# A decoder layer on one Trainium2 core: rows of q and k stacked through memory, the first LayerNorm's rows spread over steps, the cross turn one step later

## The reference

```
x = x + self_attention(layernorm(x))        # Wq, Wk, Wv with biases; 32 query heads, 16 key/value heads of 32, causal
x = x + cross_attention(layernorm(x), ctx)  # no weights; 32 query heads on 8 context heads, 64 context rows, added mask
x = x + ffn(layernorm(x))                   # silu(x Wg^T) * (x Wu^T) Wd^T, hidden size 3584, weights in 4-bit codes x scales
```

## Time and profile before

| | us |
|---|---|
| median of 3 runs (lowest to highest) | 3028.31 (3022.53 to 3028.32) |
| profiled execution, own time | 3025.31 |
| its span | 3023.5 |
| TensorE busy in the span | 2642.9 (87%) |
| VectorE, ScalarE, GpSimd busy | 2079.2, 1569.8, 1225.7 |
| attention, until the last batch's cross part ends | about 1176 |

### The profile page before, as it was taken

One profiled execution on the slowest core, in us unless ns is written; L12 is line 12 of the kernel. 1 busy time (PEld: TensorE's weight loads), 2 busy tenths in 40 slices (PEclk: granted clock), 3 DMA queues, 4 the chain that ended last, 5 costly groups with the idle time before them and its releaser, 6 DMA issues.

```text
span 3023.5 us, 52802 instructions
## 1 busy us (share of the span) xinstructions
PE 2642.9 (87%) x18464; PEld 1414.6 (47%) x18464; DVE 2079.2 (69%) x2844; ACT 1569.8 (52%) x2794; POOL 1225.7 (41%) x1068
## 2 busy tenths in 40 slices
PE   5878877886888653599999999999999999999999
PEld 2555554555655442344444444444444444444444
DVE  5455456546655657687786887878878788787872
ACT  3445444444554534674564745646556465474650
POOL 2345444544554634242442433424334243342430
PEclk9988988997999767799999999999999999999999
DMA  4121112222211214111111211112111111121112
GB/s 157 37 77 45 46 55 65 65 67 66 57 49 50 68 55 140 55 63 47 56 49 42 69 35 56 56 42 63 42 49 56 43 62 49 42 63 42 56 38 111
DMA packets 149813, 180.20 MB, mean 60 GB/s; under 512 B 39920, under 2 KB 91632, under 8 KB 149616
## 3 DMA queue, kind: packets, MB, share of 16 engines
q1 hardware_dynamic: 149616, 177.83, 19.0%
HBM read 132.00 MB, written 25.17 MB: 52 GB/s over the span
## 4 chain that ended last, share of the span: by engine, by line
PE 56%; DVE 2%; issue 1%; ACT 1%; DMA 1%; POOL 0%; SPq 0%; DVEq 0%; ACTq 0%; POOLq 0%
PE f_bank L1462 36%; PE f_down L1482 19%; DVE line L1586 1%; DMA codes<-in_codes 1%; DVE f_stats L1600 0%; DVE fT_l L1613 0%; ACT line L1511 0%; ACT f_xn L1522 0%; ACT fT_h L1530 0%; PE f_down L1444 0%; DVE w L1592 0%; ACT line L1508 0%; DVE h L1622 0%; DVE y L1627 0%; DVE f_mean_var L1603 0%
## 5 line engine op out<-in xcount | busy, mean ns | idle before, releaser
L1586 DVE TENSOR_TENSOR line<-line 128x512 f32<-128x512 f32 x1008 | 928.8, 972 | 43.7 <-issue 29.1
L1511 ACT ACTIVATE line<-codes 128x512 f32<-128x512 int32 x1008 | 590.8, 620 | 386.0 <-DVE line L1586 288.0
L1462 PE MATMUL f_bank<-fT_h,up_h 128*128 128x512 f16 x1792 | 680.9, 380 | 4.3 <-DVE fT_l L1613 3.0
L1462 PE MATMUL f_bank<-fT_l,up_h 128*128 128x512 f16 x1792 | 680.7, 380 | 0.0
L1462 PE MATMUL f_bank<-fT_h,up_l 128*128 128x512 f16 x1792 | 680.4, 380 | 0.0
L510 POOL TENSOR_TENSOR p_l<-p,p_h 128x512 f16<-128x512 f32 x320 | 372.0, 1172 | 452.6 <-ACT p_h L920 451.6
L912 ACT ACTIVATE p<-bank 128x512 f32<-128x512 f32 x320 | 190.6, 596 | 462.7 <-PE bank L704 462.4
L1074 DVE TENSOR_REDUCE block_max<-bank 128x4 f32<-128x512 f32 x320 | 218.7, 686 | 273.2 <-PE bank L675 270.5
L1627 DVE SCALAR_TENSOR_TENSOR y<-f_down,y 128x1024 f32<-128x1024 f32 x224 | 274.3, 1224 | 190.9 <-PE f_down L1482 190.9
L1392 POOL TENSOR_TENSOR up_l<-w,up_h 128x512 f16<-128x512 f32 x112 | 145.0, 1295 | 530.4 <-ACT up_h L1516 530.4
L1387 POOL TENSOR_TENSOR w<-w,scales 128x512 f32<-128x512 f32 x168 | 263.8, 1570 | 227.4 <-DVE w L1592 227.4
(11 more groups left out here) (159 smaller groups left out, 4535.3 us busy)
## 6 DMA issues: line engine op xcount, KB each, us to landing
codes<-in_codes SPq DMA_DIRECT2D x168, 256.0 KB, 3.0
scales<-in_scales SPq DMA_DIRECT2D x336, 128.0 KB, 2.9
xn<-in_x SPq DMA_DIRECT2D x16, 512.0 KB, 4.5
q_rows<-nat_h SPq DMA_DIRECT2D x256, 32.0 KB, 1.9
x_unit<-in_x SPq DMA_DIRECT2D x64, 128.0 KB, 2.7
x<-x_unit SPq DMA_DIRECT2D x64, 128.0 KB, 2.2
y<-x SPq DMA_DIRECT2D x4, 2048.0 KB, 12.8
out<-y SPq DMA_DIRECT2D x16, 512.0 KB, 2.6
```

What stands on the lines that cost most here:

```text
L1462: mm = nc.tensor.matmul(bank[(GATE, UP)[kind] + n % 2][:, :], w[:, chunk, kind, P * c:P * c + P], x[:, c, cols], start=(m == 0), stop=(m = ...
L1511: op = nc.scalar.activation(line[:, m, :], codes[:, slot, :], ACT.Copy, scale=slope, bias=intercept)
L1586: nc.vector.tensor_tensor(line[:, n + 2, :], line[:, n, :], line[:, n + 2, :], ALU.max)\
```

## The change

It has four parts.

1. **Stacking.** `nat` holds both parts of a kind side by side. SyncE stores it as one transfer (`store_nat`, 128 rows x 2 KB) to a tensor in memory, waits, and loads the stacked rows with 3 transfers of 128 KB (32 rows x 4 pairs x 1 KB).
2. **LayerNorm's rows.** `turn_in(s)` replaces `last_turn` and the `FIRST_*` tables. For batch 1 rows are turned in steps 1, 3, 5 and 7 of batch 0; for batch 2 in steps 9 and 13 of batch 0 and 1 and 5 of batch 1; for batch 3 one batch later. A block is turned into `x1T` and stored (`store_turned`, 512 KB) to memory; in i = 9 the four blocks are loaded into `xT` (`load_turned`, 4 x 512 KB) once the batch's projections are done. `xT` is now laid out by block, high and low, column block: a projection's moving operand `xT[:, :, half, c, :]` has four runs of 128 columns. `KINDS_AT` moves a kind: steps 5, 6, 7 have one each and step 8 has one.
3. **Cross turn.** `x_turn`, `x_high_part` and `x_low_part` of piece y = s - 21 stand in chunks 1, 1 and 2 of step s, a step after its scores; `x_weigh` in chunk 3, the output at the end of VectorE's step; the exponential in chunk 3. `T_OF` swaps banks to fit.
4. **Around these.** `p32` has 3 buffers for 4. The x2 store moves from i % 4 = 0 to 1, on GpSimd the shift and the root stand behind more low parts, and at the start all four blocks of rows are loaded and normalised before the weights are cut.

```diff
-        S_OF, T_OF = (0, 0, 1, 0, 1), (1, 1, 0, 1, 0)
+        S_OF, T_OF = (0, 0, 1, 0, 1), (0, 1, 0, 1, 1)
...
-        KINDS_AT = {0: (6,), 1: (7,), 2: (8,), 3: (9,), 4: (10, 11), 5: (12, 13), 6: (14,), 7: (15,)}
+        KINDS_AT = {0: (6,), 1: (7,), 2: (8,), 3: (9,), 4: (10, 11), 5: (12,), 6: (13,), 7: (14,), 8: (15,)}
...
+        def turn_in(s):
             b, i = divmod(s, NP)
+            if 0 < b < B and i % 4 == 3:
+                return "cross", b - 1, i // 4
+            if b == 0 and i in (1, 3, 5, 7):
+                return "first", 1, i // 2
+            if 0 <= b < B - 2 and i in (9, 13):
+                return "first", b + 2, i // 4 - 2
+            if 0 < b < B - 1 and i in (1, 5):
+                return "first", b + 1, 2 + i // 4
+            return None
...
+            def load_turned(b):
+                sp.wait_ge(turned_stored, 16 * TURNED_BY[b])
+                sp.wait_ge(proj_done, NP * b)
+                for i in range(QT):
+                    sp.dma_start(xT[:, i, :, :, :].rearrange("p a c n -> p (a c n)"), dram["xT"][b % 2, i, :, :])\
+                        .then_inc(turned_loaded, 16)
...
+            def store_nat(q):
+                u, kind = q // 4, q % 4
+                sp.wait_ge(proj_low, 3 * u + kind + 1)
+                if u >= 2:
+                    sp.wait_ge(rows_stacked[kind], 16 * 3 * (u - 1))
+                sp.dma_start(dram["nat"][u % 2, kind, :, :], nat[:, kind, :, :].rearrange("p a t -> p (a t)"))\
+                    .then_inc(nat_stored[kind], 16)
...
             def stack_rows(u, kind):
                 if kind == 0 and u >= 2:
                     sp.wait_ge(t_scored, CHUNKS * PAIRS * (u - 1))
-                sp.wait_ge(proj_low, 3 * u + kind + 1)
-                for j in range(4):
-                    for r in range(3):
-                        ...
-                        sp.dma_start(dst, src[D * j:D * j + D, kind, :]).then_inc(rows_stacked[kind], 16)
+                sp.wait_ge(nat_stored[kind], 16 * (u + 1))
+                for r in range(3):
+                    half = (0, 0, 1)[r] if kind == 0 else (0, 1, 0)[r]
+                    ...
+                    src = dram["nat"][u % 2, kind, :, T * half:T * half + T].rearrange("(j d) t -> d j t", d=D)
+                    sp.dma_start(dst, src).then_inc(rows_stacked[kind], 16)
...
                     if k == 1:
                         if s % 2 == 0 and 0 <= s < NS:
                             turn_max(s // 2)
-                        y = crossed(s - 1 - X_LAG, s)
                         if y is not None:
-                            if y >= 1:
-                                pe.wait_ge(x_read, y)
-                            x_weigh(y, XO_BANK, px_h, px_l)
+                            pe.wait_ge(t_exp, min(CHUNKS * (s - 1) + 3, CHUNKS * NS))
+                            if y >= 1:
+                                pe.wait_ge(x_low, y)
+                            x_turn(y, T_BANK + XT_OF, s32[:, y % 2, :])
...
-                    if k == 3 and x is not None:
-                        ...
-                        x_turn(x, T_BANK + XT_OF, s32[:, x % 2, :])
+                    if k == 3 and y is not None:
+                        if y >= 1:
+                            pe.wait_ge(x_read, y)
+                        x_weigh(y, XO_BANK, px_h, px_l)
...
             def exps(f):
                 act.wait_ge(t_scored, f + 1)
-                if f >= 4:
-                    act.wait_ge(p_low, f - 3)
+                if f >= 3:
+                    act.wait_ge(p_low, f - 2)
...
+                    if turn_in(s + 1) and k == 1:
+                        turn_stats(turn_in(s + 1))
+                    if turn_in(s + 1) and k == 4:
+                        ln_normal(LN_AT[turn_in(s + 1)], turn_row(turn_in(s + 1)))
+                if y is not None:
+                    x_out(y, XO_BANK)
```

More of the change, by code:

```diff
@@ L468, in _ @@
             sp.dma_start(t.mask[:, :, :], dram["mask"].rearrange("(r p) t -> p r t", p=P)).then_inc(small_loaded, 16)
-            for n in range(4, 10):
+            for n in range(2, 8):
+                if n < 4:
+                    sp.wait_ge(ln_xn, n + 1)
                 load_w(n)
@@ L472, in _ @@
                 step(s)
-                if s >= FROM:
-                    load_w(16 + s)
+                for n in range(2):
+                    if 8 + 2 * (s - FROM) + n < NW:
+                        load_w(8 + 2 * (s - FROM) + n)
             for u in range(2):
@@ L600, in _ @@
                 if n < NX:
-                    shift(x, p32[:, x % 4, :])
+                    shift(x, p32[:, x % 3, :])
                 if n >= 2:
@@ L645, in project @@
                             pe.wait_ge(w_low, 4 * g + piece + 1)
-                        for m, (w, x) in enumerate(((t.w_h, xT_h), (t.w_h, xT_l), (t.w_l, xT_h))):
-                            mm = nc.tensor.matmul(dst[:, :], w[:, c, cols], x[:, c, :],
+                        for m, (w, half) in enumerate(((t.w_h, 0), (t.w_h, 1), (t.w_l, 0))):
+                            mm = nc.tensor.matmul(dst[:, :], w[:, c, cols], xT[:, :, half, c, :],
                                                   start=(c == 0 and m == 0), stop=(c == CT - 1 and m == 2))
@@ L651, in project @@
                     for c in range(CT):
-                        for m, (w, x) in enumerate(((t.w_h, xT_h), (t.w_h, xT_l), (t.w_l, xT_h))):
-                            mm = nc.tensor.matmul(dst[:, rows], x[:, c, rows], w[:, c, cols],
+                        for m, (w, half) in enumerate(((t.w_h, 0), (t.w_h, 1), (t.w_l, 0))):
+                            mm = nc.tensor.matmul(dst[:, rows], xT[:, piece, half, c, :], w[:, c, cols],
                                                   start=(c == 0 and m == 0), stop=(c == CT - 1 and m == 2))
@@ L1053, in nat_low @@
                 dve.wait_ge(proj_high, 3 * u + kind + 1)
-                nc.vector.tensor_tensor(nat_l[:, kind, :], proj32[:, q % 2, :], nat_h[:, kind, :],
+                nc.vector.tensor_tensor(nat[:, kind, 1, :], proj32[:, q % 2, :], nat[:, kind, 0, :],
                                         ALU.subtract).then_inc(proj_low, 1)
@@ L1173, in step, with row_normal @@
                     cut_context(b)
-            for i in range(4):
-                first_stats(0, i)
-                first_normal(0, i)
-                if i:
-                    cut_w(i - 1)
-                    first_low(0, i - 1)
-            cut_w(3)
-            first_low(0, 3)
+            def row_normal(i):
+                row = xn[:, i, :] if i < 2 else x_row[:, i - 2, :]
+                dve.wait_ge((row_loaded, late_loaded)[i // 2][i % 2], 16)
+                ln_stats(i, row)
+                ln_normal(i, row)
+            row_normal(0)
+            row_normal(1)
+            for i in range(2):
+                row_low(i)
+                row_normal(2 + i)
+            row_low(2)
+            cut_w(0)
+            row_low(3)
+            for n in range(1, 4):
+                cut_w(n)
             dve.wait_ge(small_loaded, 48)
@@ L1198, in _ @@
                     if n == -2:
+                        x_low_part(LATE_X - 1, T_BANK + XT_OF, px_h, px_l)
+                    ln_normal(at, last_row[rt])
+                    if n == -2:
                         x_out(LATE_X - 1, XO_BANK)
-                    ln_normal(at, last_row[rt])
                 if 0 <= n < 4:
-                    rows = slice(P * n, P * n + P)
                     for half in range(2):
-                        ln_low_part(LN_AT["cross", B - 1, n], half, PROJ_BANK + half, xT_h[:, :, rows], xT_l[:, :, rows])
+                        ln_low_part(LN_AT["cross", B - 1, n], half, PROJ_BANK + half, xT[:, n, :, :, :])
                 if 0 <= n < NX:
-                    if n >= 4:
-                        dve.wait_ge(x_turned, x - 3)
-                    x_soft(x, S_BANK + x % 2, p32[:, x % 4, :])
+                    if n >= 3:
+                        dve.wait_ge(x_turned, x - 2)
+                    x_soft(x, S_BANK + x % 2, p32[:, x % 3, :])
                 if 1 <= n <= NX:
```

309 lines of the change are left out of this document (145 added, 164 removed).

## The result

The changed kernel takes 2860.55 us (median of 4 runs, 2857.48 to 2863.15) against 3028.32 of the kernel before beside it: a ratio of 0.9451, with a 95% interval of 0.944 to 0.9463. Forecast was 2852, with 2820 to 2925 as its range. The profiled execution took 2857.48, and its page begins as follows; the answers to it are the earlier trace rows.

A forecast was written before the change was run, and what follows sets the result against it. TensorE bounds undisturbed steps; the rest is stalls. Steps 1 to 18 -45, 20 to 55 -111, 56 to 64 -10, start -9, end 0: 3025.3 - 175 = 2850, 2852 with part of the median's 3 us; range 2820 to 2925.

The forecast's parts named there:

- second kinds: Steps 20 to 55: a second projection kind in a step adds 5.2 us, three times, 15.6 together.
- px_l behind low part and statistics: Cross steps where low part and statistics fall together: px_l 1.7 us late in 7 of 36, 12 us.
- Idleness left, 0.4 a step: Steps 20 to 55: 0.4 of the 1.0 us TensorE idleness stays in every step, 14.4 us.
- The reload: Step 9: 2 MB load issued 5 to 8 us in; stalls 9, 10, 10, plus 2.5 each for half clock.
- Rival (b): Reload twice as long, as x1 stores, x2 stores and row loads share the engines: 2889 us; chance 0.07.
- Rival (d): VectorE order costs more than it gives, px_l 1.7 us late in all 36 steps: 2902 us; chance 0.08.
- no wait of VectorE's statistics for a row: Sign of a right forecast: row loads go out two steps ahead, so VectorE's 11.65 us row wait is gone.
- The context keys: Cross steps: K values gain a store ahead of them; no stall, except 2 us once in the first.
- The chain of the stacking: One store and three loads of a kind, two landings in series: 6.7 us by rows, 6.2 by the skill.
- Rival (a): Stacking gains nothing; two landings and small pieces take the time of 12 issues: 2918 us; chance 0.10.
- rival (c): Projections read the moving operand slower in runs of 128 columns; at twice the time 3101 us; chance 0.04.
- The end: Cross parts after step 64 form one chain of engines; a turn is moved: 0, bounds -5 to +5.

The follow-up runs named there:

- the experiment: VectorE's row statistics moved from chunk 1 to chunk 2, behind px_l, against the changed kernel: 2836.66 us, ratio 0.9359.
- the last experiment: Context-key transfers put ahead of the store of a kind, against the changed kernel with statistics behind px_l and reload in two halves: 2816.89 us, ratio 0.9308.
- the spreading alone: Changed kernel with stacking and cross turn as before, so only LayerNorm's rows are spread, timed against the kernel before: 3000.61 us, ratio 0.9915.

## Why the prediction was right, and where its terms were off

The total is 0.3% off, and the mechanism was the one given: TensorE bounds an undisturbed step, all else is stalls with places, and most of them come out of the SyncE queue. That the total came so close is in part luck, as the table shows. The stretch with the largest term, by its own parts (steps 20 to 55; measured lengths of the steps named less 11.75 each):

| part | forecast | measured |
|---|---|---|
| plain steps with their cross turns, idleness left | 431.1 + 14.4 | 36 x 11.75 + 9 x 0.65 = 428.9 |
| second kinds (20, 36, 52) | 15.6 | 20.6 |
| two reloads with their steps 9 (25, 26, 41, 42) | 25 - 4.4 = 20.6 | 12.4 |
| px_l behind low part and statistics (22, 24, 28, 32, 38, 54) | 12 | 15.2 |
| more row turns | 6 | 1.5 |
| steps 34, 50 | 0 | 11.9 |
| steps 30, 46 | 0 | 9.0 |
| steps 21, 37, 53 | 0 | 9.5 |
| sum | 500 | 509.1 |

Three rows are too large by 29 us together, the others too small, or missing, by 39; the sum is 9 off.

**Idleness left, 0.4 a step: too much.** Both short waits went entirely in the plain steps. I had kept 14.4 us for waits I might miss; the plain steps have 0.16 us of idleness each.

**The reload: the issue right, the landing too long.** Forecast were stalls of 9, 10 and 10 us, measured 6.1, 5.1 and 2.9. The transfer was asked for when the forecast said, but the last of the 2 MB landed 9.5, 10.7 and 9.5 us after the first issue and not 12.8. The row that I took was one transfer of 2 MB; this is four of 512 KB. Steps 10, 26 and 42 last 7.8, 6.7 and 5.6 us more than a plain one of their batch. The stall itself is 6.1, 5.1 and 2.9 of it; the remaining 1.7, 1.6 and 2.7 (forecast 2.5) go with a lower granted clock, 0.81, 0.82 and 0.74 in the three steps. That the two steps 9 of this stretch would be 2.2 us shorter each was wrong: they take 11.5 and 12.0, with px_l 1.8 and 1.3 late. The 10.5 from which the prediction took its 9.5 and 10.2 for a step 9 divides by 9 readings a stretch that holds 8 steps (56 to 63), so it should have been 11.8. The 9.5 held all the same (9.3), the 10.2 did not. Rival (b), a reload twice as long, did not happen.

**px_l: right in size and place.** 1.7 late was forecast, 1.8 to 1.9 measured, in six steps where seven were counted. Rival (d), the order on VectorE as a cost in every step, did not happen; a part of it did, 23.9 us by the experiment, of which the forecast had 12.

**The x1 row: missed.** The prediction looked at the queue for the reload, the stacked rows and the context keys, and never asked when the x1 row lands for the statistics that now stand ahead of px_l. The prediction named "no wait of VectorE's statistics for a row" as a sign that it was right, and this sign failed: they wait for an x1 row 8.1 us in 3. It has the pattern of the earlier trace rows again, 3.09 us for 11.65, and with TensorE behind it 12 us in two steps.

**Steps 30 and 46, and 21, 37, 53: missed.** In 30 and 46 TensorE waits for a block maximum (2.6 and 2.2) and then px_l (0.4 and 2.1); the context cut is on VectorE ahead of that maximum. Step 14 has the same wait (2.5). In 21 and 37 it waits 1.4 for a projected value's first addition on VectorE. No experiment took these apart.

**The context keys.** "Nothing, 2 us once in the first cross step" was close on the wait (1.2 in step 20, 2.0 in step 36) but these two land in the steps with two kinds, and the last experiment shows 4.7 us for them.

**The chain of the stacking: right.** Forecast 6.7. The third kind ahead of step 50:

```profile
728.09 0.34 SPq L391 DMA_DIRECT2D nat_parts<-nat  x1
730.12 1.45 SPq L406 DMA_DIRECT2D q_rows<-nat_parts  x3
```

The loads go out 2.0 us after the store, as soon as it has landed (2.0 by its row, below the 2.7 taken), the last of them near 731.1, and with 3.1 for its landing the chain is 6.1 us. The Trainium skill ("DMA: Bandwidth & Descriptors", Anatomy of one DMA) had it at an estimated 6.2, and this trace agrees; the section describes transfers issued from GpSimd, these are SyncE's. The store at 502.57 shown further up is an exception: fifteen of the sixteen increments of its semaphore came 2.0 us after the issue, the last at 506.29, 3.7 after, and only then could the loads go. 40 of the 48 stores landed within 2.4 us; six of the other eight stand before step 9, at 3.4 to 6.1. No q_rows wait stands in a step with a cross part; the three that are left are ahead of step 1 (6.8) and in steps 2 and 6 (2.9 and 0.4), where three of 1 to 1.5 were forecast. Rival (a), that stacking gains nothing, is refuted: 125.9 us alone.

**The moving operand in pieces** (rival (c)) costs nothing: 0.215 against 0.216 us. The rule of the Trainium skill named with it ("SBUF — State Buffer", Door 1) agrees.

**Which part gave how much** the prediction had wrong in its wording. It put the loss in the two LayerNorm steps down to where LayerNorm stood. The runs say that stacking alone takes 13.4 of the 22.2 us in steps 24 and 25, and that the spreading alone is worth 25.3 of the whole.

**The end.** Forecast 0, measured -5, inside the bounds given. What in the last cross part gave it was not followed.

## What to carry to other kernels

Count what an in-order DMA queue issues before you look at bytes: twelve issues of 0.6 to 0.7 us delayed rows, values and row loads that looked like stalls of the engines that waited for them, and cutting 576 issues to 192 (144 loads and 48 stores) gave three quarters of the gain. Before you move a load or store on such a queue, list what each neighbour waits for, since an early place behind a waiting instruction is a late one, and a place ahead of others makes them late. When work is moved out of a stall, look one step on: the spreading without a free queue carried most of a stall, some 20 us, from one step to the next.

## What the runs showed of the hardware that was not expected

- Issuing the same 32 KB transfer costs SyncE 0.52 us from memory and 0.69 from the core's own buffers in the mean (12 in 6.27 us against 7.55, 8.16 and 8.92).
- Four loads of 512 KB, issued over 2.0 us, had landed 9.5 us after the first issue in two batches and 10.7 in the third, sooner than one transfer of 2 MB of another tensor (12.8 before, 11.8 in the changed kernel's list). No run loaded the same rows both ways.
- Cutting such a load in two halves by what is read first took off 5 us in two of the three steps (26: 18.5 to 13.2, 42: 17.4 to 12.3), of which the shorter wait is 3.4 and 2.9. The rest goes with the clock: in step 42 the granted clock is 0.74 with the stall and 0.93 without.
- A transfer's semaphore is raised in sixteen increments, and one of them can be late by itself: at 502.57 fifteen came 2.0 us after the issue and the last 3.7. A load that waits for all sixteen is late with it. In four of the later kernels the same store, in step 33, landed 3.1 to 4.2 us after its issue, again with the other fifteen increments at 2.0. Why was not followed.
